# Two message groups and the carry of a part ahead of the sixteen target-score products of the part after next

## The chip, the cores and the metric

The kernel runs on one core of one Trainium2 chip. The time is the device time of one execution in microseconds (us). The engines of the core are named as in the profile: PE is TensorE, with PEld for its weight loads; DVE is VectorE; ACT is ScalarE; POOL is GpSimd; SP is SyncE, which only issues transfers. Each works through its own list of instructions in order, and semaphores tie the lists together.

## What is computed

The reference is a network of two graph layers over 3125 nodes and 100000 edges, which are sorted by target. The change touches one part of the second layer only, the attention over edges:

```python
h_src = h_all[edge_type, src]
h_dst = h_all[edge_type, dst]
scores = jnp.einsum('ehd,hd->eh', h_src, attn_src) + jnp.einsum('ehd,hd->eh', h_dst, attn_dst)
scores = jnp.where(scores > 0, scores, NEG_SLOPE * scores)
amax = jnp.maximum(jax.ops.segment_max(scores, dst, num_segments=n), 0.0)
w = jnp.exp(scores - amax[dst])
denom = jax.ops.segment_sum(w, dst, num_segments=n) + 1e-12
w = w / denom[dst]
msg = h_src * w[..., None]
out = jax.ops.segment_sum(msg, dst, num_segments=n)
```

So each edge fetches a row of 256 numbers and 8 scores of its source (by edge type), adds 8 scores that belong to its target, and its weighted row is summed into its target.

## The kernel before

The edges are cut into 28 parts (`NPART`) of 28 chunks (`PART`) of 128 edges. Seven groups (`MG`) of four chunks (`MGRP`) make a part. The function `attend` runs all of it, with one hand-written order for each engine; the order on PE is a loop over `p` from -1 to 27, in which three parts are in flight at once:

- **POOL** gathers the source rows of a part, one indirect transfer (L2213) for each chunk, into one of three buffers (`RING = 3`; in the trace they bear the names `relations_or_ring`, `tables_or_ring`, `xn_or_ring`). From the fourth part on it may start group q of part p+3 only when PE has used up group q of part p in the same buffer: it waits for the semaphore `used` ahead of every fourth gather.
- **PE, target scores** (`own_scores(p + 2, ...)`, L2353): 28 small products for each part (128x64 each), a one-hot of the targets times the score table of the near nodes, into the accumulator `po`. Those of groups 0, 1 and 2 stand between other work, those of groups 3 to 6 (16 products) stand in one piece behind `flip_back`. The last one raises the semaphore `own_sum`.
- **DVE, target scores** (`own_scores(n + 1)`, L2455 to L2469): waits for `own_sum`, picks the scores of the edge's type out of `po`; then `scores` (L2479, L2482) adds the source's scores and raises what PE's `flip` (L2361) of the next round waits for.
- **Maxima by target**: `flip`, `to_row`, `to_column`, `flip_back` (L2361, L2368, L2372, L2377) move the scores between layouts through PE, and DVE scans them (L2494 to L2513). `below_greatest` (L2525 to L2528) reads what `flip_back` turned, ACT takes the exponentials (L2320, L2322), and DVE weighs the gathered rows with them (`weigh`, L2544, seven instructions of 1.2 us), which are the messages of the next `p`.
- **PE, messages** (`messages(p, q)`, L2390): four products (128x264) for each group q, one-hot times weighted rows, summed in `acc`. The last product of a group raises `used`. `add_carry` (L2395) adds the row carried from the part before and raises `summed`; ACT copies the total out (`keep_total`, L2331); `take_last` (L2400) picks the row to carry on, behind a wait for that copy and for the weighing.
- **SP** loads the targets and the near rows of part p+3 and stores the totals.

Each product in fp32 stands in the trace as two matmuls with a weight load each, so 16 products are 32 matmuls and 32 loads, and a message group is 8 matmuls.

A stage ahead of the attention matters for the argument too: a dense mixing of the nodes (names `mix_...`), in which PE's products L2007 are read by DVE's L2050, and nothing else stands between the two. POOL already gathers the first two parts of the attention during it.

Of the kernel before, what the change touches and what calls it, by code (L numbers as in the profile page):

```python
# [2217 lines left out]
def attend(g, name, c, near_rows, targets, sums, gaps, gather, ahead, oh, masked):  # L2218
# [8 lines left out]
    with ExitStack() as ctx:  # L2227
# [40 lines left out]
        def slots(p):  # L2268
            return gather.slots[p % RING]
# [4 lines left out]
        with nc.Block() as block:  # L2274
            @block.gpsimd
            def _(pl):
                for n in range(ahead, NC):
                    p, j = n // PART, n % PART
                    if j % MGRP == 0 and p >= RING:
                        pl.wait_ge(used, (p - RING) * MG + j // MGRP + 1)  # L2280
                    gather.fetch(n)
# [57 lines left out]
            @block.tensor  # L2339
            def _(pe):  # L2340
                def own_scores(p, *groups):
                    if p >= NPART:
                        return
                    for q in groups:
                        if q == 0:
                            pe.wait_ge(near_in[p % 2], 16 * (p // 2 + 1))
                            pe.wait_ge(ohT_ready, 2 * p + 1)
                            if p:
                                pe.wait_ge(own_ready, p)
                        if q == half // MGRP:  # L2350
                            pe.wait_ge(ohT_ready, 2 * p + 2)
                        for j in range(q * MGRP, (q + 1) * MGRP):
                            mm = nc.tensor.matmul(po[:, j // bank, j % bank * sc:(j % bank + 1) * sc],  # L2353
                                                  ohT[:, j * P:(j + 1) * P], near[:, p % 2, :], start=True, stop=True)
                        if q == MG - 1:
                            mm.then_inc(own_sum, 1)

                def flip(p):
                    pe.wait_ge(st_ready, p + 1)
                    for k in range(2):  # L2360
                        mm = nc.tensor.transpose(pseq[0:PH, k * P:(k + 1) * P],  # L2361
                                                 st[:, p % 2, k, :, :].rearrange("p h r -> p (h r)"), c.ident)
                    mm.then_inc(turned, 1)

                def to_row(p, k):
                    pe.wait_ge(ends, 2 * p + k + 1)
                    end = (2 * P - 1, 0)[k]
                    nc.tensor.transpose(prow, s[:, end:end + 1], c.ident[0:PH, 0:PH]).then_inc(row_out, 1)  # L2368

                def to_column(p, k):  # L2370
                    pe.wait_ge(into_in, 2 * p + k + 1)
                    nc.tensor.transpose(pcol, into, c.ident[0:1, 0:1]).then_inc(col_out, 1)  # L2372

                def flip_back(p):
                    pe.wait_ge(scanned, p + 1)
                    for k in range(2):
                        mm = nc.tensor.transpose(pback[:, k * PH:(k + 1) * PH], s[:, k * P:(k + 1) * P],  # L2377
                                                 c.ident[0:PH, 0:PH])
                    mm.then_inc(back, 1)

                def messages(p, q):
                    n = p * MG + q
                    if q == 0:
                        pe.wait_ge(share_ready, p + 1)
                        if p:
                            pe.wait_ge(total_ready, p)
                    pe.wait_ge(oh_ready, n + 1)
                    pe.wait_ge(msg_ready, n + 1)
                    for j in range(q * MGRP, (q + 1) * MGRP):
                        mm = nc.tensor.matmul(acc[:, 0:RW], oh[:, j, :], slots(p)[:, j, :], start=j == 0, stop=False)  # L2390
                    mm.then_inc(used, 1)

                def add_carry(p):
                    pe.wait_ge(carry_ready, p + 1)
                    nc.tensor.matmul(acc[:, 0:RW], c.ident[0:1, 0:P], carry, start=False, stop=True).then_inc(summed, 1)  # L2395

                def take_last(p):
                    pe.wait_ge(total_ready, p + 1)
                    pe.wait_ge(msg_ready, MG * min(p + 2, NPART))
                    nc.tensor.matmul(pcar[0:1, 0:RW], c.part_last[:, p:p + 1], total, start=True, stop=True  # L2400
                                     ).then_inc(carried, 1)

                def nothing(*_):
                    pass
                gaps.turn_flag(pe, pseq)
                own_scores(0, *range(MG))
                for p in range(-1, NPART):
                    more = p + 1 < NPART
                    of_this = messages if p >= 0 else nothing
                    if more:  # L2410
                        flip(p + 1)
                    own_scores(p + 2, 0)
                    of_this(p, 0)
                    if more:
                        to_row(p + 1, 0)
                    of_this(p, 1)
                    if more:
                        to_column(p + 1, 0)
                    own_scores(p + 2, 1)
                    of_this(p, 2)  # L2420
                    if more:
                        to_row(p + 1, 1)
                    of_this(p, 3)
                    if more:
                        to_column(p + 1, 1)
                    own_scores(p + 2, 2)
                    of_this(p, 4)
                    if more:
                        flip_back(p + 1)
                    own_scores(p + 2, 3, 4, 5, 6)  # L2430
                    of_this(p, 5)
                    of_this(p, 6)
                    if p >= 0:
                        add_carry(p)
                        take_last(p)

            @block.vector
# [866 lines left out]
```

## Time and profile before

| what | value |
|---|---|
| median of 3 runs | 4177.66 us (4175.0 to 4179.73) |
| the profiled execution | 4138.91 us, of which the span of the trace is 4137.3 us |
| mean granted TensorE clock | 0.856 of full |
| PE busy, PEld, DVE, ACT, POOL | 79%, 58%, 50%, 19%, 26% of the span |
| attention over edges | about 2465 to 3640 us of the span |

The profiled execution is 38.75 us below the median of the runs. The trace gives every instruction a start and a length in us from the start of the span. Behind a row may stand in brackets how long the engine was idle before it and what ended that; this releaser is inferred, and "issue" or "remote" mean that the profile names none. A clock of 1.00 is 2.4 GHz and 0.50 is 1.2 GHz.

### The profile page before, as it was taken

What the parts mean: (1) busy time and instruction counts of PE and PEld (TensorE: products, weight loads), DVE (VectorE), ACT (ScalarE), POOL (GpSimd) and SP (SyncE); (2) the same over time, 40 slices, a digit from 0 to 9 for tenths busy, and PEclk for the clock granted to TensorE, in tenths of its full rate; (3) what the DMA queues carried; (4) which work ended last, traced back from release to release, by engine and by line L of the source; (5) the groups of instructions that cost most, each with busy time, mean ns of one, the idle gap of its engine ahead of it and who ended that gap; (6) DMA issues with size and microseconds to landing.
All of it is one profiled execution on the core that took longest, in us unless ns stands there. A gap on an engine that the chain in (4) does not pass through costs nothing. (4 is left out here: it accounts for less than half of the span.)

```text
span 4137.3 us, 48378 instructions
## 1 busy us (share of the span) xinstructions
PE 3278.1 (79%) x14155; PEld 2397.1 (58%) x14156; DVE 2076.4 (50%) x5104; ACT 801.6 (19%) x1602; POOL 1066.4 (26%) x1103
## 2 busy tenths in 40 slices
PE   3899979979989546999939954767777777759998
PEld 2666668868867525888825443545454545535555
DVE  7999923323334540000167625666666766743333
ACT  0122212222222322332213310000000000022222
POOL 3800000000000033000030055666666666300000
PEclk9999989989999757999969965767676767779999
DMA  2722255534420024212152233444444444210000
GB/s 79 276 107 95 96 133 130 130 109 127 127 63 0 0 70 113 76 56 91 45 102 119 111 97 92 123 114 124 114 124 116 123 121 117 66 59 8 16 8 31
DMA packets 306810, 383.86 MB, mean 93 GB/s; under 512 B 40199, under 2 KB 249841, under 8 KB 303249
## 3 DMA queue, kind: packets, MB, share of 16 engines
q1 hardware_dynamic: 239456, 218.36, 16.9%
q0 software_dynamic: 50992, 146.13, 12.3%
q10 hardware_dynamic: 16256, 18.10, 1.4%
q8 instruction: 50, 0.82, 0.1%
q14 instruction: 56, 0.45, 0.0%
HBM read 270.97 MB, written 111.53 MB: 92 GB/s over the span
## 5 line engine op out<-in xcount | busy, mean ns | idle before, releaser
L496 PE MATMUL counts_acc<-onehot_lo,onehot_key 128*128 128x400 bf16 x2000 | 363.4, 337 | 45.4 <-DVE onehot_key L478 45.3
L2213 POOL DMA_INDIRECT relations_or_ring<-relation_rows,table_row x280 | 278.2, 994 | 412.8 <-SPq L1987 258.7
L475 DVE TENSOR_SCALAR onehot_lo<-node_ids,source_lo 128x800 bf16<-128x800 int16 x1000 | 358.1, 453 | 0.0
L496 PEld LDWEIGHTS counts_acc<-onehot_lo,onehot_key 128*128 128x128 bf16 x2000 | 268.1, 139 | 144.7 <-DVE onehot_key L478 84.7
L607 PE MATMUL agg_agg<-xn_or_ring,agg_slab 128*128 128x257 f32 x1250 | 278.3, 382 | 26.2 <-DMA agg_slab<-edge_counts 26.2
L607 PE MATMUL agg_agg<-x_gnn,agg_slab 128*128 128x257 f32 x1250 | 277.2, 381 | 18.9 <-DMA agg_slab<-edge_counts 18.9
L2213 POOL DMA_INDIRECT tables_or_ring<-relation_rows,table_row x252 | 251.1, 996 | 143.8 <-issue 71.6
L2213 POOL DMA_INDIRECT xn_or_ring<-relation_rows,table_row x252 | 251.2, 997 | 112.7 <-issue 71.9
L607 PEld LDWEIGHTS agg_agg<-xn_or_ring,agg_slab 128*128 128x128 f32 x1250 | 238.5, 191 | 61.9 <-DMA agg_slab<-edge_counts 26.3
L607 PEld LDWEIGHTS agg_agg<-x_gnn,agg_slab 128*128 128x128 f32 x1250 | 237.7, 190 | 54.9 <-DMA agg_slab<-edge_counts 19.7
L2353 PE MATMUL att_po<-att_near,att_onehotT 128*128 128x64 f32 x1568 | 229.5, 306 | 29.9 <-issue 23.5
L2390 PE MATMUL att_acc<-relations_or_ring,mixing_or_onehot 128*128 128x264 f32 x560 | 192.8, 474 | 73.6 <-issue 69.1
L1239 DVE TENSOR_SCALAR ffn_xe<-ffn_pt,xn_or_ring 128x256 f32<-128x256 f32 x60 | 29.9, 540 | 422.2 <-PE ffn_pt L1200 422.2
L2353 PEld LDWEIGHTS att_po<-att_near,att_onehotT 128*128 128x128 f32 x1568 | 215.9, 220 | 39.6 <-issue 32.2
L2390 PE MATMUL att_acc<-tables_or_ring,mixing_or_onehot 128*128 128x264 f32 x504 | 170.4, 468 | 72.5 <-issue 67.3
L1214 PE MATMUL ffn_ph<-ffn_xe,wide_w 128*128 128x256 f32 x960 | 218.1, 385 | 9.0 <-ACT ffn_h L1256 7.6
L2390 PE MATMUL att_acc<-xn_or_ring,mixing_or_onehot 128*128 128x264 f32 x504 | 171.6, 468 | 67.1 <-issue 58.0
L1223 PE MATMUL ffn_py<-wide_w,ffn_h 128*128 128x256 f32 x960 | 215.8, 383 | 5.1 <-ACT ffn_h L1256 5.1
L1214 PEld LDWEIGHTS ffn_ph<-ffn_xe,wide_w 128*128 128x128 f32 x960 | 185.0, 193 | 37.4 <-ACT ffn_h L1256 10.0
L1223 PEld LDWEIGHTS ffn_py<-wide_w,ffn_h 128*128 128x128 f32 x960 | 181.0, 191 | 34.4 <-issue 10.9
L641 DVE TENSOR_SCALAR agg_inv<-agg_agg 128x1 f32<-128x1 f32 x50 | 7.9, 158 | 377.6 <-PE agg_agg L607 377.6
L2390 PEld LDWEIGHTS att_acc<-relations_or_ring,mixing_or_onehot 128*128 128x128 f32 x560 | 122.5, 230 | 127.8 <-issue 109.6
(450 smaller groups left out, 5209.8 us busy)
## 6 DMA issues: line engine op xcount, KB each, us to landing
agg_slab<-edge_counts SPq DMA_DIRECT2D x50, 1600.0 KB, 7.9
edge_counts<-counts_out SPq DMA_DIRECT2D x100, 400.0 KB, 2.3
relation_rows<-tables_or_ring SPq DMA_DIRECT2D x25, 1056.0 KB, 3.9
att_targets<-targets SPq DMA_DIRECT2D x28, 896.0 KB
wide_w<-L_ffn_W ACTq DMA_DIRECT2D x14, 1024.0 KB, 7.0
expert_rows_in<-blank_rows POOLq DMA_DIRECT2D x34, 256.0 KB
expert_rows_out<-blank_rows POOLq DMA_DIRECT2D x33, 256.0 KB
ffn_xin<-expert_rows_in SPq DMA_DIRECT2D x31, 256.0 KB
```

The source lines that it names most:

```text
L475: nc.vector.tensor_scalar(oh_lo[:, k, j, :], c.nodes[:, 0:LO], lo[:, ds(at + j, 1)], None, ALU.is_equal)
L496: mm = nc.tensor.matmul(acc[:, k, h, 0:HALF_LO], oh_key[:, k, :, j], oh_lo[:, k, j, h * HALF_LO:(h + 1) * HALF_LO], start=False, stop=Fals ...
L607: mm = nc.tensor.matmul(pa[:, b, 0:D + 1], slab[:, b, k * P:(k + 1) * P], xn[:, k, 0:D + 1], start=(k == 0), stop=(k == NT - 1))
L641: link(nc.vector.tensor_scalar(inv[:, b, 0:1], pa[:, b, D:D + 1], 1.0, None, ALU.max))
L1214: mm = nc.tensor.matmul(ph[:, m % 4, 0:UNIT], w1s[:, b, k, m * P:(m + 1) * P], xe[:, k, :], start=(k == 0), stop=(k == KT - 1))
L1223: mm = nc.tensor.matmul(py[:, s, 0:D], h[:, m, s * P:(s + 1) * P], w2s[:, b, m, :], start=(m == 0), stop=(m == mt - 1))
L1239: ins = nc.vector.tensor_scalar(xe[:, k, :], pt[:, k * UNIT:(k + 1) * UNIT], ln[0][:, k, ds(e, 1)], ln[1][:, k, ds(e, 1)], ALU.mult, ALU.add)
L2213: self.nc.gpsimd.indirect_dma_start(self.slots[p % RING][:, j, :], None, self.rows_of, bass.IndirectOffsetOnAxis(ap=self.c.row[:, n:n + 1] ...
L2353: mm = nc.tensor.matmul(po[:, j // bank, j % bank * sc:(j % bank + 1) * sc], ohT[:, j * P:(j + 1) * P], near[:, p % 2, :], start=True, sto ...
L2390: mm = nc.tensor.matmul(acc[:, 0:RW], oh[:, j, :], slots(p)[:, j, :], start=j == 0, stop=False)
```

## The change

In each round of PE's loop the products of groups 3 to 6 of part p+2 no longer stand directly behind `flip_back(p + 1)`, but behind the message groups 5 and 6 of part p and its carry. Nothing is added or removed, and no wait is new; the lists of the other engines are the same.

```diff
                     of_this(p, 4)
                     if more:
                         flip_back(p + 1)
-                    own_scores(p + 2, 3, 4, 5, 6)
                     of_this(p, 5)
                     of_this(p, 6)
                     if p >= 0:
                         add_carry(p)
+                    own_scores(p + 2, 3, 4, 5, 6)
+                    if p >= 0:
                         take_last(p)
```

The list of PE in the first full round of the loop (p = 0), before. `att_po` is the accumulator of the target scores, `att_acc` that of the messages, `att_pseq` the bank through which scores are turned, `att_pshare` takes the row to carry on:

```order
L2390 MATMUL att_acc<-relations_or_ring0,mixing_or_onehot 128x264 x4
L2377 MATMUL att_pseq<-ident,att_scan 128x112 x2
L2353 MATMUL att_po<-att_near,att_onehotT 128x64 x16
L2390 MATMUL att_acc<-relations_or_ring0,mixing_or_onehot 128x264 x8
L2395 MATMUL att_acc<-att_carry,ident 128x264
L2400 MATMUL att_pshare<-att_total,part_last 1x264
L2361 MATMUL att_pseq<-ident,att_scores 112x128 x2
```

The same place on PE in the changed kernel:

```order
L2390 MATMUL att_acc<-relations_or_ring0,mixing_or_onehot 128x264 x4
L2377 MATMUL att_pseq<-ident,att_scan 128x112 x2
L2390 MATMUL att_acc<-relations_or_ring0,mixing_or_onehot 128x264 x8
L2395 MATMUL att_acc<-att_carry,ident 128x264
L2353 MATMUL att_po<-att_near,att_onehotT 128x64 x16
L2400 MATMUL att_pshare<-att_total,part_last 1x264
L2361 MATMUL att_pseq<-ident,att_scores 112x128 x2
```

The 16 products moved behind nine others; `take_last` and the next `flip` stand where they stood. The last round with such products (p = 25, where POOL has nothing left to gather), before:

```order
L2377 MATMUL att_pseq<-ident,att_scan 128x112 x2
L2353 MATMUL att_po<-att_near,att_onehotT 128x64 x16
L2390 MATMUL att_acc<-tables_or_ring1,mixing_or_onehot 128x264 x8
L2395 MATMUL att_acc<-att_carry,ident 128x264
L2400 MATMUL att_pshare<-att_total,part_last 1x264
```

And in the changed kernel:

```order
L2377 MATMUL att_pseq<-ident,att_scan 128x112 x2
L2390 MATMUL att_acc<-tables_or_ring1,mixing_or_onehot 128x264 x8
L2395 MATMUL att_acc<-att_carry,ident 128x264
L2353 MATMUL att_po<-att_near,att_onehotT 128x64 x16
L2400 MATMUL att_pshare<-att_total,part_last 1x264
```

The same swap stands in all 26 rounds from p = 0 to p = 25. In round -1 there are no messages, and in rounds 26 and 27 no target scores, so nothing moves there.

## Rows read from the trace of the kernel before

**Rows 1.** Page, busy time (share of the span) and instructions of each engine

```profile
PE 3278.1 (79%) x14155; PEld 2397.1 (58%) x14156; DVE 2076.4 (50%) x5104; ACT 801.6 (19%) x1602; POOL 1066.4 (26%) x1103
```

**Rows 2.** Waits from 2565 to 3575: engine, line, waited for; total us, times, longest

```profile
DVE relations_or_ring L2463 <- remote: 169.5, 25, 7.1
...
DVE att_greatest L2525 <- remote: 76.2, 23, 4.5
```

**Rows 3.** Timeline of POOL, one part: start, length, engine, line, transfer, count, idle before

```profile
3042.69 0.94 POOL L2213 DMA_INDIRECT relations_or_ring<-relation_rows,table_row  x1 [1.39 <-PE att_acc L2390]
...
3067.15 0.94 POOL L2213 DMA_INDIRECT relations_or_ring<-relation_rows,table_row  x1 [0.30 <-issue]
3071.41 0.94 POOL L2213 DMA_INDIRECT relations_or_ring<-relation_rows,table_row  x1 [3.32 <-DMA xn_or_ring<-L_ffn_ln_b_t]
...
3083.63 0.95 POOL L2213 DMA_INDIRECT tables_or_ring<-relation_rows,table_row  x1 [1.41 <-PE att_acc L2390]
```

**Rows 4.** Timeline of PE and DVE in the same part, round p = 12

```profile
3052.07 0.36 PE L2377 MATMUL att_pseq<-ident,att_scan 112*128 112x112 f32 x2
...
3052.26 3.70 PE L2353 MATMUL att_po<-att_near,att_onehotT 128*128 128x64 f32 x32
...
3054.77 0.39 DVE L2525 TENSOR_SCALAR att_greatest<-att_pseq 128x224 f32<-128x224 f32 x1 [3.71 <-remote]
...
3056.18 0.38 PE L2390 MATMUL att_acc<-relations_or_ring,mixing_or_onehot 128*128 128x264 f32 x1 [0.23 <-issue]
...
3056.47 8.01 DVE L2544 TENSOR_TENSOR tables_or_ring<-tables_or_ring,att_pshare 128x1024 f32<-128x1024 f32 x7
...
3057.61 0.47 PE L2390 MATMUL att_acc<-relations_or_ring,mixing_or_onehot 128*128 128x264 f32 x1 [1.04 <-issue]
...
3069.53 3.08 PE L2390 MATMUL att_acc<-relations_or_ring,mixing_or_onehot 128*128 128x264 f32 x5 [0.59 <-issue]
...
3071.15 1.28 DVE L2463 TENSOR_TENSOR relations_or_ring<-att_po,att_of_type 128x448 f32<-128x448 f32 x2 [6.37 <-remote]
...
3077.04 0.68 PE L2361 MATMUL att_pseq<-ident,att_scores 128*112 128x128 f32 x2 [1.76 <-DVE att_scores L2482]
...
3080.26 3.10 PE L2390 MATMUL att_acc<-tables_or_ring,mixing_or_onehot 128*128 128x264 f32 x8
```

**Rows 5.** Timeline of round p = 25, behind POOL's last gather

```profile
3572.36 1.43 POOL L2213 DMA_INDIRECT relations_or_ring<-relation_rows,table_row  x1 [0.30 <-issue]
...
3584.74 3.70 PE L2353 MATMUL att_po<-att_near,att_onehotT 128*128 128x64 f32 x32
...
3586.64 8.01 DVE L2544 TENSOR_TENSOR xn_or_ring<-xn_or_ring,att_pshare 128x1024 f32<-128x1024 f32 x7
...
3588.28 3.78 PE L2390 MATMUL att_acc<-tables_or_ring,mixing_or_onehot 128*128 128x264 f32 x16
...
3594.99 1.28 DVE L2463 TENSOR_TENSOR relations_or_ring<-att_po,att_of_type 128x448 f32<-128x448 f32 x2
```

**Rows 6.** Timeline of the mixing stage, with POOL's first and last gather in it

```profile
2382.74 0.94 POOL L2213 DMA_INDIRECT relations_or_ring<-relation_rows,table_row  x1 [258.72 <-SPq L1987]
...
2411.91 2.07 PE L2007 MATMUL mix_po<-mixing_or_onehot,mix_stT 128*128 128x256 f32 x4 [7.34 <-issue]
...
2422.68 0.42 DVE L2050 TENSOR_TENSOR mix_h<-mix_po,mixing_or_onehot 128x256 f32<-128x256 f32 x1 [15.21 <-DMA coll_got<-expert_rows_out,slots]
...
2431.48 0.95 POOL L2213 DMA_INDIRECT tables_or_ring<-relation_rows,table_row  x1 [0.30 <-issue]
```

**Rows 7.** Windows: length, busy us (count) of PE, PEld, DVE, ACT, POOL, clock

```profile
3042.00:3058.00 16.00, 14.73 (x90) 12.16 (x89) 10.54 (x23) 1.14 (x3) 11.87 (x12) 1.00 0.49 154
3059.00:3082.00 23.00, 15.32 (x32) 7.61 (x32) 16.16 (x22) 0.99 (x4) 15.42 (x16) 0.50 0.36 98
...
sum 40.90, PE 31.04 PEld 20.66 DVE 27.70 ACT 2.13 POOL 28.29; mean PE 10.35 PEld 6.89 DVE 9.23 ACT 0.71 POOL 9.43
```

## The prediction

> **What bounds the kernel now.** The page comes first: PE is busy for 79% of the span and nothing else is over 58% [rows 1]. Such a share says little about one stage, so the next views are the waits and the timeline of the attention, the only stage in which the change moves anything.
>
> One part takes 40.94 us there: POOL starts on a new part's rows at 3042.69 and again at 3083.63 [rows 3]. No engine fills that: in three windows that cover it (40.90 us, the sum row) PE is busy for 31.04 us, POOL for 28.29 and DVE for 27.70 [rows 7]. It is a chain between engines. Follow one part [rows 4]. PE turns the scores back at 3052.07 and runs the 16 target-score products, 32 matmuls, from 3052.26 to 3055.96. DVE weighs the messages from 3056.47 to 3064.48. Then DVE should find the target scores ready, 8 us old; but it picks them up at 3071.15, after 6.37 us of idle time whose releaser the profile can't name. From there the chain runs on: PE's next `flip` at 3077.04 (5.9 us later), message group 0 from 3080.26, POOL's next part at 3083.63. The same wait stands in 25 parts, 169.5 us in all [rows 2]. So a part is 9.4 us from POOL's new part to `flip_back`, 19.1 from there until `own_sum` reaches DVE, and 12.5 from there to POOL's next part.
>
> The semaphore comes 15.2 us after the matmul that raises it has ended (3071.15 against 3055.96). In the same time the messages behind it crawl: 11 of the 16 matmuls of groups 5 and 6 start between 3056.18 and 3069.53 (single rows stand for the first two, nine more follow, then the x5 row), that is 1.21 us for one, where 16 of them take 3.78 us in round 25 [rows 4, 5]. What holds PE up? Three places speak.
> - Round 25 has the same burst, the same messages and the same weighing, but POOL's last gather ended at 3573.79. There the messages run at full pace and DVE goes on at 3594.99, as soon as it has weighed [rows 5]. So neither the burst nor the weighing is the cause.
> - In the mixing stage PE has next to nothing to do, but POOL gathers without a break from 2382.74 on. PE's product ended at 2413.98, and DVE, which waits for it alone, starts at 2422.68: 8.7 us late [rows 6]. So it needs POOL's gathers and no dense PE.
> - In the attention POOL gathers 20 chunks in one go, from 3042.69 to 3068.09. `flip_back` ends at 3052.43 and DVE sees it at 3054.77, already 2.3 us late; the products behind it are later. Then POOL stops, since it waits for `used` of group 5. 3.06 us after its last issue ended, PE's semaphores come through [rows 3, 4].
>
> My reading: some ten gathers into an unbroken run, what PE finishes is reported late, about 1.21 us for each matmul in order, and all that is due comes at once about 3 us after POOL stops. POOL stops because a report of PE's is held back. Before, that report is `used` of group 5, which stands behind the burst.
>
> **The change part by part.** Nothing is added or removed, so PE's work is the same; only when three semaphores are sent changes.
>
> *Message groups 5 and 6 run ahead of the burst.* They are two times 8 matmuls behind `flip_back`. At 1.21 us each from 3054.77, `used` of group 5 comes through at 3054.8 + 9.7 = 3064.5. POOL needs it at 3068.39 (3068.09 and 0.30 of issue), so POOL no longer stops there. It gathers four chunks more, at 1.25 us each (0.94 and 0.30 of issue), 5.0 us. `used` of group 6 is due at 3054.8 + 16 x 1.21 = 3074.2, and POOL needs it at 3073.4: it stops there, at 3073.1. The margin is thin: at the pace of the last eleven it holds by 0.8 us.
>
> *The burst runs behind them.* `own_sum` is again held until POOL stops. 3.06 us after 3073.1 is 3076.15, against 3071.15: **+5.0 us for each part**. By then PE has started, at the pace of before, 32 + 11 matmuls by 3069.53 and some 5.5 more, so about 48.5 of the 50 that now stand there (16 of messages, 2 of the carry, 32 of the burst). The one or two left cost **+0.4 us**.
>
> Of the count behind that, one page bears on it. PE starts 2 + 32 matmuls, with their loads 68 instructions, at full pace before the crawl sets in [rows 4]. The Trainium skill, "TensorE: Matmul & The Clock Gate", section on the architectural detail of the array, gives TensorE a queue 64 deep. By that depth 12 matmuls of the burst would pass at full pace and 3 or 4 would be left at 3076.15, some 0.8 us in place of 0.4, and the sum would be 10 us higher. No run here shows which it is.
>
> *The carry and the total.* `add_carry` runs ahead of the burst, so `summed` is sent earlier, but is held back like the others and comes through at 3076.15 at the latest; ACT's copy and `take_last` follow in 3 us, beside DVE's 5.9 us of scores. Cost nothing. If that cover were gone it would be some 1 us. `take_last` waits for the copy, and behind it stands `flip`, which waits for DVE longer.
>
> *Behind the change.* DVE's weighing (3056.47 to 3064.48) doesn't move, since `flip_back` doesn't. SP's loads of near rows wait for an `own_sum` of an earlier part and aren't late. The 8 gathers left after POOL's stop become 4, and POOL then idles until the next part: nobody waits for that. In round 25 (no gathers) the burst ends some 4.2 us later than 3588.44, still ahead of DVE's 3594.65: nothing.
>
> *The clock.* It stands at 1.00 (2.4 GHz) while PE is dense and at 0.50 (1.2 GHz) in the crawl and up to the next part [rows 7]. A longer crawl changes nothing in that; but the rise can fall a message group sooner or later, and a group takes 3.10 us at the low clock [rows 4] against 1.9 at the high one (half of the 16 in 3.78 [rows 5]). That is 1.2 us for each part to either side; I take 0, since PE's order up to there is unchanged.
>
> **The sum:** 25 parts x 5.4 us = +135 us. The profiled execution would go from 4138.91 to 4274; the median of the runs lies 38.75 us higher, which I carry over: 4177.66 + 135 = **4313 us**. With 4.2 and 6.6 us for each part it is 4283 to 4343.
>
> **The rivals.**
> - *Faster: the lateness belongs to what stands behind the burst.* If the crawl comes of the 16 message matmuls queued behind 32 dense ones, then with only `take_last` behind them `own_sum` comes in time, DVE's 6.4 us are gone, and POOL becomes the bound: 28.29 us of gathers and 28 x 0.30 of issue, 36.7 us. That is -4.2 us x 25 = -105, so 4073. It decides from the point where `own_sum` comes before the weighing ends. For it: in this stage the late ones all have messages behind the burst. Against it: round 25 and the mixing stage [rows 5, 6]. The Trainium skill speaks for this side too: the same page, section on oscillation, advises to put matmuls in one piece so that PE stays at its high clock, and the change does that. The trace agrees that dense stretches have the high clock [rows 7], but the wait isn't PE's pace. 15%.
> - *POOL stops at group 5 as before* (reports slower than 1.70 us each, (3068.4 - 3054.8) / 8). Then `own_sum` is late only by what PE has left at 3071.15, some 5.5 matmuls or 1.3 us: +33, 4210. 8%.
> - *POOL never stops* (reports come faster, under 1.16 us). It gathers all 28, 10.0 us longer, and the two longest gathers add about 1: 25 x 10 to 11 = +250 to +275, 4428 to 4453. The thin margin above speaks for it, and parts may be mixed. 13%.
> - *The change does nothing*: the held reports come free by something other than POOL's stop, at the same time as before. 4178. 9%.
>
> **How the numbers follow.** The forecast has 55%. Slower are it, the second and the third rival, 76%; faster 15%; no difference 9%. About 0.2% (8 us) is what a measurement of this kernel can tell from none. The range for 8 in 10 leaves out the faster rival and the upper end of the third: 4172 to 4440. The forecast's own range is 4283 to 4343.
>
> **What would show it.** In the profile after: DVE's wait before L2463 grows from 6.4 to about 12 us in 25 parts; POOL runs 24 gathers without a break, stops for about 3.5 us and has 4 left; matmuls of L2390 run at full pace behind L2377, and L2353 crawls; parts are 46 us apart. Wrong, if `own_sum` arrives before the weighing ends (the first rival), if POOL still stops behind 20 gathers (the second), or if it has no stop but that between parts (the third).

## The result, and the profile after

The change makes the kernel slower: the changed kernel takes 4375.43 us in the median of four runs (4358.29 to 4383.24), the kernel before beside it 4176.33 us (4167.3 to 4179.73). The ratio is 1.0475, with a 95% interval of 1.0439 to 1.0511; that is 199 us. The profiled executions are 4378.99 us and 4138.91 us, 240 us apart. These two are no clean pair: the trace after belongs to one of the four timed runs and lies 3.6 us above their median, while the trace before lies 28 us below the fastest of its four (4167.3) and within the range of chip E below (4136.52 to 4144.33). It may come from another chip than the timed runs. Some 37 of the 240 us (4176.33 less 4138.91) may thus not be the change's.

Forecast were 4313 us, +135. The sign and the place were right, the size was too small, and the experiments below add a condition that the prediction knew nothing of: on four of the five chips that I met later PE's work is seen in time, and on the one of these four on which the changed kernel itself ran it costs nothing.

In the changed kernel DVE's lines of the attention are one higher: L2464 (reads `own_sum`'s products), L2526 (behind `flip_back`), L2545 (weighing). The waits from 2575 to 3825, DVE's and POOL's lines, as in [rows 2]:

```profile
DVE relations_or_ring L2464 <- remote: 264.9, 24, 17.9
DVE att_greatest L2526 <- remote: 168.8, 24, 13.3
...
POOL relations_or_ring L2213 <- PE att_acc L2390: 96.1, 8, 16.3
POOL tables_or_ring L2213 <- PE att_acc L2390: 95.3, 8, 15.9
POOL xn_or_ring L2213 <- PE att_acc L2390: 92.0, 8, 15.7
```

DVE's wait for `own_sum` grew from 169.5 us to 264.9 (and 13.0 in one part in which PE's line is named); its wait behind `flip_back` grew from 76.2 to 168.8, which the prediction took to be unmoved. POOL, which rested 1.4 us between parts [rows 3], now idles 11.8 us (283.4 us in 24 waits).

The first and the last weighing with gathers around it, in DVE's timeline:

```profile
2574.10 8.01 DVE L2545 TENSOR_TENSOR tables_or_ring<-tables_or_ring,att_pshare 128x1024 f32<-128x1024 f32 x7
...
3825.57 8.01 DVE L2545 TENSOR_TENSOR xn_or_ring<-xn_or_ring,att_pshare 128x1024 f32<-128x1024 f32 x7
```

They are 25 parts apart: 50.06 us for each, where it was 40.92 by the same count. The parts are uneven now (39 to 62 us from weighing to weighing). One of them, to be laid beside [rows 3, 4], from the timelines of POOL, PE and DVE:

```profile
3367.97 0.95 POOL L2213 DMA_INDIRECT tables_or_ring<-relation_rows,table_row  x1 [10.76 <-PE att_acc L2390]
...
3392.10 0.94 POOL L2213 DMA_INDIRECT tables_or_ring<-relation_rows,table_row  x1 [0.30 <-issue]
3395.95 0.94 POOL L2213 DMA_INDIRECT tables_or_ring<-relation_rows,table_row  x1 [2.91 <-DMA xn_or_ring<-L_ffn_ln_b_t]
...
3404.71 0.95 POOL L2213 DMA_INDIRECT tables_or_ring<-relation_rows,table_row  x1 [0.30 <-issue]
3421.32 0.94 POOL L2213 DMA_INDIRECT xn_or_ring<-relation_rows,table_row  x1 [15.66 <-PE att_acc L2390]
```

```profile
3377.34 0.36 PE L2377 MATMUL att_pseq<-ident,att_scan 112*128 112x112 f32 x2
3377.54 3.74 PE L2390 MATMUL att_acc<-tables_or_ring,mixing_or_onehot 128*128 128x264 f32 x16
3381.20 0.71 PE L2395 MATMUL att_acc<-att_carry,ident 1*128 1x264 f32 x2
3381.84 2.20 PE L2353 MATMUL att_po<-att_near,att_onehotT 128*128 128x64 f32 x15
3385.84 0.22 PE L2353 MATMUL att_po<-att_near,att_onehotT 128*128 128x64 f32 x1 [1.80 <-issue]
3387.97 0.27 PE L2353 MATMUL att_po<-att_near,att_onehotT 128*128 128x64 f32 x1 [1.91 <-issue]
...
3395.70 0.27 PE L2353 MATMUL att_po<-att_near,att_onehotT 128*128 128x64 f32 x1 [1.13 <-issue]
3396.40 2.59 PE L2353 MATMUL att_po<-att_near,att_onehotT 128*128 128x64 f32 x11 [0.43 <-issue]
...
3417.22 3.83 PE L2390 MATMUL att_acc<-xn_or_ring,mixing_or_onehot 128*128 128x264 f32 x8
```

```profile
3381.65 0.39 DVE L2526 TENSOR_SCALAR att_greatest<-att_pseq 128x224 f32<-128x224 f32 x1 [5.31 <-remote]
...
3383.34 8.01 DVE L2545 TENSOR_TENSOR xn_or_ring<-xn_or_ring,att_pshare 128x1024 f32<-128x1024 f32 x7
...
3408.10 1.28 DVE L2464 TENSOR_TENSOR relations_or_ring<-att_po,att_of_type 128x448 f32<-128x448 f32 x2 [16.45 <-remote]
```

The messages run at full pace, 16 in 3.74 us. 15 of the burst's 32 matmuls do so too; the next ones start 2.1 us apart. In this part POOL still stops behind 20 gathers (3393.04), not behind 24. By then 13 of the burst's matmuls haven't started (the last two singles and the x11 row). The x11 row runs when POOL has already begun its last 8 gathers, and DVE sees `own_sum` at 3408.10, 2.4 us after the last of those 8 has ended (3405.66) and 9 us after the burst.

The parts aren't alike in where POOL stops (idle for over 0.6 us within a part). In 12 of the 25 it is behind 20 gathers alone, as here. In 8 it goes on to 24, as forecast, in 3 of these with a short stop behind 20 as well. In the other 5 it stops behind 16, and in 3 of these behind 20 too. But the parts in which it goes on to 24 take 49.2 to 53.4 us, not the 46 of the forecast.

### The profile page after: what moved, and what is told of

Same layout as the page of the kernel before. It is cut to its first block and busy times, and to the rows that moved or that the text cites. A ratio compares the mean times of both kernels' runs of the same rounds, so it can differ in the third digit from the quotient of the medians.

```text
span 4377.3 us, 48378 instructions
## 1 busy us (share of the span) xinstructions
PE 3237.7 (74%) x14155; PEld 2438.6 (56%) x14156; DVE 2078.5 (47%) x5104; ACT 802.2 (18%) x1602; POOL 1016.5 (23%) x1103
## 5 line engine op out<-in xcount | busy, mean ns | idle before, releaser
L2353 PE MATMUL att_po<-att_near,att_onehotT 128*128 128x64 f32 x1568 | 299.3, 332 | 326.1 <-issue 319.2
L2353 PEld LDWEIGHTS att_po<-att_near,att_onehotT 128*128 128x128 f32 x1568 | 278.3, 252 | 350.3 <-issue 349.2
L496 PE MATMUL counts_acc<-onehot_lo,onehot_key 128*128 128x400 bf16 x2000 | 365.3, 338 | 46.0 <-DVE onehot_key L478 45.9
L2213 POOL DMA_INDIRECT tables_or_ring<-relation_rows,table_row x252 | 242.2, 961 | 223.8 <-PE att_acc L2390 95.3
L2464 DVE TENSOR_TENSOR relations_or_ring<-att_po,att_of_type 128x448 f32<-128x448 f32 x112 | 69.9, 624 | 294.7 <-remote 278.7
L2361 PE MATMUL att_pseq<-ident,att_scores 128*112 128x128 f32 x56 | 18.9, 441 | 236.9 <-DVE att_scores L2483 193.2
L1849 PE MATMUL tab_po<-relations_or_ring,tables_or_ring 128*128 128x512 f32 (+1 forms) x500 | 187.6, 530 | 0.0
L731 POOL TENSOR_TENSOR x_residual<-x_residual,agg_z 128x256 f32 (+1 forms) x25 | 18.1, 726 | 661.4 <-issue 385.8
```

The lines of the kernel that those rows point to most:

```text
L496: mm = nc.tensor.matmul(acc[:, k, h, 0:HALF_LO], oh_key[:, k, :, j], oh_lo[:, k, j, h * HALF_LO:(h + 1) * HALF_LO], start=False, stop=Fals ...
L1849: mm = nc.tensor.matmul(po[:, at % depth, 0:w], stT[:, t % 2, k, :], wt[:, k, n * MMN:n * MMN + w], start=(k == 0), stop=(k == KT - 1))
L2213: self.nc.gpsimd.indirect_dma_start(self.slots[p % RING][:, j, :], None, self.rows_of, bass.IndirectOffsetOnAxis(ap=self.c.row[:, n:n + 1] ...
L2464: ins = nc.vector.tensor_tensor(masked[:, b * bank:(b + 1) * bank, :].rearrange("p n (h r) -> p n h r", h=HD), po[:, 2 * a + b, 0:bank * s ...
```

## The experiments

Theory T, as predicted: an unbroken run of POOL's indirect gathers makes PE's finished work visible late, and it comes free some 3 us after POOL stops. Rivals: the burst or what stands behind it is the cause; any transfer of POOL's is; a short stop frees nothing. Twelve runs were made, on five chips: A (e1 to e4), B (e5, e6), C (e8, e9, e11), D (e12) and E (e7, e10). "Before" is always the kernel before on the same chip.

**e1 and e2: no gathers, in both orders.** In e1 (order of before) and e2 (new order) POOL's loop reads

```diff
-                    gather.fetch(n)
+                    if p < RING:
+                        gather.fetch(n)
```

> The order of before; POOL's gathers of the attention from part 3 on are left out (DVE does not wait for them, the messages are old rows of the ring), so nothing else of PE's, DVE's or ACT's work changes. Theory (PE's reports are late because POOL gathers): own_sum follows its matmul at once in all parts, DVE's wait before L2463 is gone, a part takes what the gather-free ones take in the profile of before (28.4 us from weighing to weighing, 3586.64 to 3615.01), that is 25 x (40.96 - 28.4) = 314 us less, some 3860 us. Rival (the lateness comes of the messages queued behind the burst): own_sum stays 15 us late and the time stays within 50 us of 4178.

> The same with the order of after. Theory: without gathers the order is worth next to nothing: the last round of after takes 28.8 us against 28.4 of before, so 0.4 x 25 = 10 us over the kernel before without gathers, some 3870 us. Rival (the new order itself costs time, as the burst now ends 3.6 us later): 25 x 3.6 = 90 us over it, some 3950 us; or the first rival of the prediction, under which this order is the faster one.

Measured: 3877.34 us and 3878.53 us; parts of 33.0 us in both; DVE never waits at L2463's place. The order is worth nothing. But the kernel before took 3944.04 us on this chip, not 4178 (ratio of e1 0.9832, 0.9816 to 0.9849). So nearly all of what I had booked on the gathers was absent on chip A in the kernel before too. The step of 314 us was wrong there, and the run can't speak for T. (28.4 us a part, the round that I had gone by, has no later part to work on.)

**e3: a stop in POOL's run.**

```diff
+                    if j == 12 and p >= RING:
+                        pl.wait_ge(msg_ready, (p - RING + 1) * MG + 3)
                     gather.fetch(n)
```

> The order of before; before the 13th gather of each part POOL also waits for three weighed groups of the running part, a semaphore of DVE's. That breaks POOL's run some 15.0 us into it and lasts until some 17.4, 2.4 us. Theory (what is held comes free about 3 us after POOL stops): own_sum comes at +18, before the weighing ends at +21.8, DVE's 6.4 us are gone, POOL becomes the bound with 36.7 + 2.4 us; a part takes 38 to 39.5 us in place of 40.96, 25 x 1.5 to 3 = 37 to 75 us less: 4100 to 4140. Rival (PE's reports crawl at a pace of their own and a short stop frees nothing): the stop is added to POOL's work, same or up to 60 us slower, 4178 to 4240.

3944.44 us against 3944.04, ratio 0.9998 (0.9988 to 1.0008): nothing, since nothing was late.

**e4 and e6: plain transfers for gathers,** in the new order and in the old one.

```diff
-                    gather.fetch(n)
+                    nc.gpsimd.dma_start(gather.slots[p % RING][:, j, :], gather.rows_of[ds(n % 200 * P, P), :]
+                                        ).then_inc(landed[p % RING], 16)
```

> The order of after; POOL's gathers from part 3 on are plain transfers of 128 rows that lie together, with the same bytes and the same semaphores (other rows, so the messages are not those of the reference). If the lateness comes of the bytes that arrive or of POOL issuing transfers at all, own_sum stays late and parts stay near 50 us, 4375. If it comes of the indirect form, own_sum is on time and a part takes 29 to 36 us: 3870 to 4050. The theory leans to the second.

> The order of before with plain transfers in place of POOL's gathers from part 3 on (same bytes and semaphores, other rows). The five runs so far were on chips on which PE's reports are never late (before 3944 and 3942 us). On such a chip this gives 3877 us, as with the order of after, and says nothing more. On a chip where the kernel before takes some 4178 us it decides: if the indirect form makes the reports late, own_sum is on time in the attention and a part takes 33.5 us, 25 x 7.4 = 186 us less, some 3990; if any transfer of POOL's does, it stays at 4178.

3876.58 us on chip A and 3877.58 on chip B (before there 3941.20): the same as without any transfers, in either order.

**e5: the changed kernel as it is, once more,** on chip B.

> The changed kernel as it is. In the four runs before this one the kernel before took 3944 us on their chip, where it took 4178 on the first one, and PE's reports were not late there. If this run is on such a chip, the lateness and with it the loss must be gone: without it the order costs what it cost without gathers, 0 to 10 us, so 3944 to 3954 against 3944. If the kernel before takes some 4178 us beside it, the loss of 199 us comes again, 4375.

3941.65 us against 3941.65; ratio 0.9998 (0.9989 to 1.0008). On this chip the loss of 199 us is gone altogether. This is the only later run of the changed kernel itself. From its timelines:

```profile
3088.69 0.36 PE L2377 MATMUL att_pseq<-ident,att_scan 112*128 112x112 f32 x2
3088.89 3.74 PE L2390 MATMUL att_acc<-xn_or_ring,mixing_or_onehot 128*128 128x264 f32 x16
3089.09 0.39 DVE L2526 TENSOR_SCALAR att_greatest<-att_pseq 128x224 f32<-128x224 f32 x1 [1.40 <-PE att_pseq L2377]
...
3093.19 3.79 PE L2353 MATMUL att_po<-att_near,att_onehotT 128*128 128x64 f32 x32
...
3099.12 1.28 DVE L2464 TENSOR_TENSOR relations_or_ring<-att_po,att_of_type 128x448 f32<-128x448 f32 x2
...
3108.10 0.54 DVE L2480 TENSOR_TENSOR att_scores<-tables_or_ring,att_own 128x224 f32<-128x224 f32 x1 [4.13 <-DMA tables_or_ring<-relation_rows,table_row]
```

The burst runs whole, `flip_back` is seen at once, and the target scores are taken right behind the weighing. POOL's gathers go on without a break and at the same pace (most start 1.25 us apart, 28 take 36.5 us); from part 9 on they set the time, 36.5 us a part, and DVE waits for rows.

**e7: the burst between groups 5 and 6,** on chip E, where the kernel before takes 4139.42 us.

```diff
-                    own_scores(p + 2, 3, 4, 5, 6)
                     of_this(p, 5)
+                    own_scores(p + 2, 3, 4, 5, 6)
                     of_this(p, 6)
```

> The 16 target-score products stand between message groups 5 and 6: half of the change. On a chip on which PE's reports are not late (before some 3944) the order is worth nothing: 3936 to 3952. On one where they are (before some 4178): theory read from the trace of after (the reports come in order and slower for a message than for a product, so each message group ahead of the burst holds own_sum longer) gives about half of the loss, +90 to +110, some 4280; rival (own_sum is held until POOL stops, wherever it stands, and only the group on which POOL stops counts) gives 4178 or 4375, nothing between.

4291.42 us, ratio 1.0368 (1.0338 to 1.0398), +152; parts of 47.0 us. This lies between before and after, nearer to after than half way, and neither forecast of the expectation was met. DVE's waits from 2575 to 3700:

```profile
DVE relations_or_ring L2463 <- remote: 251.8, 22, 14.1
DVE att_greatest L2525 <- remote: 100.3, 19, 13.1
```

That it is neither 4178 nor 4375 doesn't speak against "`own_sum` is held until POOL stops". With one message group ahead of the burst POOL goes on to 24 gathers in 23 of the 25 parts. One of them, from the timelines of PE, POOL and DVE:

```profile
3463.74 0.45 PE L2353 MATMUL att_po<-att_near,att_onehotT 128*128 128x64 f32 x1 [1.15 <-issue]
...
3474.41 0.95 POOL L2213 DMA_INDIRECT tables_or_ring<-relation_rows,table_row  x1 [0.30 <-issue]
...
3479.45 1.28 DVE L2463 TENSOR_TENSOR relations_or_ring<-att_po,att_of_type 128x448 f32<-128x448 f32 x2 [12.77 <-remote]
```

The burst is done 11 us before POOL stops (3475.36), and DVE sees `own_sum` 4.1 us after that stop. This is the course that the prediction gave to the change: +6.1 us for each part here, +5.4 there. What the full change adds to it is that the burst isn't done when POOL stops.

**e8 and e9: stretches.** To have several comparisons on one chip, these kernels differ by part. e8 puts together plain transfers, e3's stop, no fetching and gathers; e9 puts the burst ahead of `flip_back`, then behind as in the change, then the stop.

> The order of before; POOL differs by stretch (while part p runs, POOL fetches part p + 3). p 0 to 6: plain transfers of the same bytes in place of gathers (other rows). p 7 to 13: gathers, and before the 13th POOL also waits for three weighed groups (a stop of some 2.4 us). p 14 to 19: no fetching at all (left out, DVE doesn't wait for it). p 20 to 24: gathers as before. On a chip where the kernel before takes some 4140 to 4180 us: theory (POOL's indirect gathers make PE's reports late and a stop of POOL's frees them): 33.5 us for each part, 38 to 39.5, 33.5, 40.96. Rival A (POOL's transfers of any form): 40.96 in the first stretch. Rival B (a chip where PE is slow to report in itself, gathers or not): 40.96 in the first and third. Rival C (a short stop frees nothing): 41 to 43.4 in the second. On a chip where it takes 3944: 33.5, 36 to 38, 33.5, 36.3.

> Whole computation, all gathers; PE's order differs by stretch. p -1 to 4: as before. p 5 to 11: the 16 target-score products ahead of flip_back. p 12 to 18: as in the changed kernel. p 19 to 25: as in the changed kernel, and POOL's run is broken before its 13th gather until three groups are weighed. On a chip with late reports: 40.96 us a part, then the burst first. If reports come in order at a pace of their own, the lateness moves from own_sum to back, which now stands behind 16 products more: DVE weighs some 10 us later, 46 to 52 us a part; rival (only what stands behind the burst is late, or only what is finished more than ten gathers into POOL's run): own_sum in time and back 2 us late, 37 to 39 us. Third stretch 50 us. Fourth: if a stop of POOL's frees the reports, 38 to 44; if it does not, 50 or more. On a chip without: 36.3 in all but the fourth, 36 to 38 there.

On chip C: 3879.54 us and 3940.60 us against 3941.74. e9's ratio is 0.9995 (0.9984 to 1.0006). That doesn't make every order free where reports are in time. The first weighings of the stretch with the burst ahead of `flip_back` and of the next one lie seven parts apart:

```profile
2629.14 8.00 DVE L2552 TENSOR_TENSOR xn_or_ring<-xn_or_ring,att_pshare 128x1024 f32<-128x1024 f32 x7
...
2888.03 8.00 DVE L2552 TENSOR_TENSOR relations_or_ring<-relations_or_ring,att_pshare 128x1024 f32<-128x1024 f32 x7
```

That is 37.0 us a part, against 33.0 in the five parts ahead and 32.9 in the five behind, which have the order of before and of the change. The kernel as a whole isn't slower because POOL's gathers run through without a stop, 36.5 us for 28, and end when they would have ended anyway.

**e10: stretches on a chip with late reports** (E; before 4139.19 us, this 4132.57). This is the run that decides.

> Both of the last two in one kernel, in shorter stretches. p 0 to 4: POOL's transfers plain in place of gathers (other rows). p 5 to 10: gathers, with the stop before the 13th until three groups are weighed. p 11 to 15: no fetching (left out, DVE doesn't wait for it). p 16 to 20: as before. p 21 to 25: the 16 target-score products ahead of flip_back, POOL as before. On a chip where the kernel before takes 4140 to 4180: theory (POOL's indirect gathers make the reports late, a stop frees them, reports come in order): 33.5, 38 to 39.5, 33.5, 40.96, 46 to 52 us a part, back some 10 us later in the last. Rival A (any transfer of POOL's): 40.96 in the first stretch. Rival B (such a chip's PE reports late with or without gathers): 40.96 in the third too. Rival C (a short stop frees nothing): 41 to 43.4 in the second. Rival D (only what runs late in POOL's run, or stands behind the burst, is late): 37 to 39 in the last. On a chip where it takes 3944: 33.5, 36 to 38, 33.5, 36.3, 36.3.

The first and a later weighing of each stretch, from DVE's timeline (4, 4, 4, 3 and 3 parts apart):

```profile
2560.74 8.01 DVE L2556 TENSOR_TENSOR tables_or_ring<-tables_or_ring,att_pshare 128x1024 f32<-128x1024 f32 x7
...
2693.73 8.01 DVE L2556 TENSOR_TENSOR xn_or_ring<-xn_or_ring,att_pshare 128x1024 f32<-128x1024 f32 x7
...
2773.49 8.01 DVE L2556 TENSOR_TENSOR tables_or_ring<-tables_or_ring,att_pshare 128x1024 f32<-128x1024 f32 x7
...
2961.75 8.01 DVE L2556 TENSOR_TENSOR xn_or_ring<-xn_or_ring,att_pshare 128x1024 f32<-128x1024 f32 x7
...
2997.37 8.01 DVE L2556 TENSOR_TENSOR relations_or_ring<-relations_or_ring,att_pshare 128x1024 f32<-128x1024 f32 x7
...
3128.72 8.01 DVE L2556 TENSOR_TENSOR tables_or_ring<-tables_or_ring,att_pshare 128x1024 f32<-128x1024 f32 x7
...
3205.45 8.01 DVE L2556 TENSOR_TENSOR relations_or_ring<-relations_or_ring,att_pshare 128x1024 f32<-128x1024 f32 x7
...
3328.37 8.00 DVE L2556 TENSOR_TENSOR relations_or_ring<-relations_or_ring,att_pshare 128x1024 f32<-128x1024 f32 x7
...
3386.29 8.01 DVE L2556 TENSOR_TENSOR tables_or_ring<-tables_or_ring,att_pshare 128x1024 f32<-128x1024 f32 x7
...
3539.66 8.01 DVE L2556 TENSOR_TENSOR tables_or_ring<-tables_or_ring,att_pshare 128x1024 f32<-128x1024 f32 x7
```

| stretch | forecast, us a part | measured | what DVE shows |
|---|---|---|---|
| plain transfers | 33.5 | 33.25 | `own_sum` in time |
| gathers, stop before the 13th | 38 to 39.5 | 47.07 | `own_sum` in time, the scans late |
| no fetching | 33.5 | 32.84 | in time |
| as before | 40.96 | 40.97 | 7.1 us of wait before L2473, as in [rows 2] |
| burst ahead of `flip_back` | 46 to 52 | 51.12 | 20 us of wait before L2537 |

Rivals A (any transfer) and B (the chip alone) fall: with the same bytes in plain transfers nothing is late, on the chip and in the execution in which gathers bring back 40.97. (The plain transfers read 128 rows that lie together, so scattered rows and the indirect form aren't told apart.) Rival D's time, 37 to 39 us, falls with the last row; e9's 4 us for this order don't fill the gap to 51. Its rows, PE first:

```profile
3365.56 3.68 PE L2359 MATMUL att_po<-att_near,att_onehotT 128*128 128x64 f32 x32
3369.07 0.36 PE L2383 MATMUL att_pseq<-ident,att_scan 112*128 112x112 f32 x2
3369.27 1.29 PE L2396 MATMUL att_acc<-relations_or_ring,mixing_or_onehot 128*128 128x264 f32 x5
...
3384.59 0.39 DVE L2537 TENSOR_SCALAR att_greatest<-att_pseq 128x224 f32<-128x224 f32 x1 [20.04 <-remote]
```

`flip_back` ends 13.2 us into POOL's run (3356.18 is its start) and is seen 15.2 us late, 3.4 us after POOL's stop at 3381.24. In the kernel before it ends 9.7 us into the run and is seen 2.3 us late. So the lateness goes by how far POOL's run has come, as the reading with some ten gathers has it; that this also puts `flip_back` behind the burst, no run takes apart.

The second stretch refuted my forecast but not the mechanism. `own_sum` came in time, since the burst fell into POOL's stop, yet a part took 47. The stop only moved POOL's run:

```profile
2872.35 0.94 POOL L2213 DMA_INDIRECT xn_or_ring<-relation_rows,table_row  x1 [8.46 <-PE att_acc L2396]
...
2902.24 0.94 POOL L2213 DMA_INDIRECT relations_or_ring<-relation_rows,table_row  x1 [0.30 <-issue]
2906.50 0.94 POOL L2213 DMA_INDIRECT relations_or_ring<-relation_rows,table_row  x1 [3.32 <-DMA xn_or_ring<-L_ffn_ln_b_t]
```

```profile
2890.72 0.26 DVE L2520 COPY att_row<-att_pseq 1x112 f32<-1x112 f32 x1 [3.49 <-PE att_pseq L2374]
...
2897.73 0.16 DVE L2512 COPY att_first<-att_pseq 112x1 f32<-112x1 f32 x1 [4.66 <-remote]
...
2906.37 0.26 DVE L2520 COPY att_row<-att_pseq 1x112 f32<-1x112 f32 x1 [6.25 <-DMA agg_slab<-edge_counts]
```

It now gathers 24 chunks in one go from 2872.35 on, and what falls late into that run are the short trips between PE and DVE of the scans. They wait 3.5, 4.7 and 6.3 us, the more the longer the run has lasted, where the same waits are 2.5 us at most in the kernel after. The stop itself lasts 8.5 us where 2.4 were forecast. The lateness went to whatever PE finishes late in POOL's run.

**e11 and e12: rests.** The new order up to p 14, the old one behind; among others three memsets ahead of the 1st, 13th and 21st gather:

```diff
+                    if 13 <= p < 23 and j in (0, 12, 20):
+                        for _ in range(3):
+                            nc.gpsimd.memset(gather.slots[p % RING][:, j:j + MGRP, :], 0.0).then_inc(rested, 1)
+                            rests += 1
+                            pl.wait_ge(rested, rests)
```

> Stretches again; the order of the changed kernel for p up to 14, the order of before from p 15 on. p 0 to 4: plain transfers in place of gathers (other rows). p 5 to 9: gathers, nothing else changed. p 10 to 14: before its 1st, 13th and 21st gather POOL rests: three memsets of 128x1056 one after the other, some 3 to 4 us by the 128x512 one of 0.73 us; no engine is waited for. p 15 to 19: the same rests with the order of before. p 20 to 24: every second chunk by a plain transfer, no rests. On a chip where the kernel before takes 4140 to 4180: theory (only unbroken indirect gathers make reports late, a rest of 3 us frees them; the order costs time only while they are late): 33.5 us a part, 50, then both orders alike at POOL's pace, 36.3 + 3 x 3.5 = 47, with own_sum under 3 us late; last stretch 37 to 41. Rival (a rest that short, or one with POOL busy on its own, frees nothing): 50 + 10 = 60 in the third and 51 in the fourth, own_sum still 9 and 15 us late. Rival (the new order costs time in itself): 37 in the first. On a chip where it takes 3944: 33.5, 36.3, 47, 47, 36.

> The same kernel as the last one, which ran on a chip without late reports (33.2, 33.2 to 36, 45.9, 45.5 and 33.3 us a part there). On a chip where the kernel before takes 4140 to 4180: theory (only unbroken indirect gathers make reports late, a rest of 3.3 us frees them; the order costs time only while they are late): 33.2, 50, 46 and 46, with own_sum under 3 us late; the last stretch 37 to 41. Rival (a rest that short, or one with POOL busy on its own, frees nothing): 50 + 10 = 60 in the third and 51 in the fourth, own_sum still 9 and 15 us late. Rival (on such a chip the new order costs time in itself): 37 in the first.

Both met chips without late reports (C and D): 3996.79 and 4000.93 us, against 3941.81 and 3940.06. The rests take 3.3 us each and both orders with them take 45.9 and 45.5 us a part, near the 47 forecast from POOL's pace; with half of the chunks by plain transfers a part takes some 33 us. What rests do on a chip with late reports stays open.

## Why the prediction was right, and where its sum failed

- **What bounds the kernel.** Right for chips with late reports, and now shown: POOL's gathers, not the burst and not the weighing (e10, all in one execution). The reading from round 25 and the mixing stage [rows 5, 6] held.
- **`used` of group 5 comes through at 3064.5, so POOL goes on to 24.** Wrong in 17 of 25 parts. It took the messages' reports at 1.21 us for a matmul, a pace read while products of 64 columns were due. With messages due first, starts lie up to 2.1 us apart and POOL mostly stops behind 20, as the second rival's condition said ("slower than 1.70 us each"). But this isn't what made the sum short, since the 8 parts with 24 gathers are no shorter; in e7, where the step holds, the price was right.
- **"About 48.5 of the 50 have started" when POOL stops.** Wrong; this is the step that failed. In the part shown 37 of the 50 have started. At full pace go 2 + 16 + 2 + 15 = 35 matmuls with their loads, 70 instructions. It is 32 to 38 in 20 of the 25 parts (21 to 26 in the other five), 32 to 41 in 23 of the 25 parts of e7, 33 to 37 in the kernel before, and with the burst first 32 + 2 + 5 = 39. So where PE is held goes by a count of instructions more than by a time. The Trainium skill, "TensorE: Matmul & The Clock Gate", section on the architectural detail of the array, has the queue 64 deep; of the two counts that I weighed the trace agrees with that one, roughly. With the rest at 2.1 us the burst wasn't done when POOL stopped.
- **+5.4 us for each part.** Measured over 23 parts of the two traces: POOL's start to `flip_back` 9.71 us (was 9.38), `flip_back` to `own_sum` at DVE 27.28 (was 19.13, forecast 24.5), from there to POOL's next start 13.07 (was 12.46): +9.1. The missing term is what follows from the two points above: the last product starts 22.4 us behind `flip_back` in the mean, so it falls near or into POOL's second run, and is seen 1.6 to 9.7 us later (4.9 in the mean). I had let the second run hold back nothing, and the term of 0.4 us for what PE had left stood in its place. 25 x 9.1 = 228 us of the 240 between the profiled executions; the first weighing already lies 8.5 us later (2537.59 against 2529.11), ahead of the parts counted. By the timed runs it is 199 / 25 = 8.0 for each part, so about 1 of the 9.1 may be the difference between the two traces' chips. The 38.75 us that I carried over have no counterpart after.
- **The clock, taken as 0.** It is the likely cause of the 0.6 us in the last leg: message group 0 now runs wholly at the low clock, 3.83 us in the part shown where it took 3.10 [rows 4].
- **`flip_back` doesn't move.** Wrong: DVE's wait for it more than doubled, 3.0 to 6.8 us a part. POOL's and PE's phases are no longer locked, and in some parts it falls late into POOL's run (up to 13.3 us of wait).
- **The second rival** (POOL stops at group 5 as before) had the right place in most parts and the wrong price: +33, since it counted only 5.5 matmuls as left and let the second run hold back nothing.
- **The range** (4172 to 4440) held 4375 because it reached to the rival in which POOL gathers all 28, which is not what happened. The forecast's own range missed.
- **What nothing foresaw: the chip.** The changed kernel itself ran on B alone, with no difference; C and D ran its order in stretches that take the same as those with the old order within 1%, A ran it without gathers. On E half of the change cost 152 us, but the change itself didn't run there. So the forecast holds for the chip of the first comparison and, by e7, for chips like E; on the others the outcome is that of no change.

A version that beats both kernels didn't come out of this: on the chips without late reports POOL's 28 indirect gathers set the time whatever PE's order is, and on E the one stop that I made (e10) moved the lateness elsewhere.

## What to carry to other kernels

When a consumer starts long after the record of its producer has ended, look at what the other engines were doing in that time, and test it by stretches within one kernel, since another run may be on another chip. A pace read while one kind of work is due doesn't hold for another, and a wait that is released when some engine stops has to be followed through that engine's next run as well. Before an order is tuned around such a lateness, time it on more than one chip.

## What the runs showed of the hardware

The same program took 3940 to 3944 us on chips A to D and 4139 on E; the chip of the first comparison, with 4176, may or may not be one of these. With late reports POOL's indirect transfers themselves keep their pace (0.94 and 0.30 us of issue on both kinds of chip); in these timelines only the waits for PE's work end late, by 15.2 us at the end of 20 gathers (in the part shown after, ACT takes up at 3382.76 what DVE ended at 3382.72, in the middle of POOL's run), and behind some 70 instructions (64 to 82 in most parts) its starts are held to steps of about 0.7 us or a multiple. The same bytes by plain transfers of rows that lie together do nothing of it (e10). What differs between the chips, why only PE is hit, and why its starts lie 2.1 us apart in one order and 0.7 to 2.1 in the others, no run here settles.
